# A four-layer block on one core: another order for the start-up work of the first two pairs

## The reference

```python
x = x + (x @ W0[expert[b]] + bias0[expert[b]])                         # 16 experts, one for a sample
x = x + (x @ W1.T + ((x @ A[ad[b]].T) @ B[ad[b]].T) * s[ad[b]])        # low-rank adapters, rank 16, 8 of them
x = x + attention(x)      # Wq, Wk, Wv, RMS norm, rotation by position, paged keys and values, window 256, Wo
x = x + (W3[subject[b]].T @ x + bias3[b])                              # mixes the 64 tokens of a sample
```

## Time and profile before

| | us |
|---|---|
| median of three runs | 952.81 |
| lowest and highest run | 951.57, 953.42 |
| span of the profiled execution (first to last instruction) | 948.6 |
| PE busy | 907.5 (96%) |
| DVE busy | 651.1 (69%) |
| POOL busy | 522.3 (55%) |
| ACT busy | 444.3 (47%) |

### The profile page before, as it was taken

How to read it: one execution, slowest core, us unless ns; L and a number is a source line. 1 busy time by engine, 2 the same in 40 slices (tenths; PEclk the granted TensorE clock), 3 DMA queues, 4 the chain that set the end, 5 groups by cost and what they waited for, 6 DMA issues and landing times.

```text
span 948.6 us, 23332 instructions
## 1 busy us (share of the span) xinstructions
PE 907.5 (96%) x6477; PEld 660.8 (70%) x6477; DVE 651.1 (69%) x1853; ACT 444.3 (47%) x1190; POOL 522.3 (55%) x502
## 2 busy tenths in 40 slices
PE   5789999999999999999997899999999999999997
PEld 3456666766666667666676777877777887787785
DVE  5345545667768774556754678777878877888875
ACT  2333333333333333333322566666666666666663
POOL 2136455464564657855556666566565665656530
PEclk9799999999999999999998799999999999999999
DMA  9978988778788787887844566666666676567741
GB/s 295 265 230 282 330 308 290 252 261 289 247 282 276 244 291 255 271 295 247 284 159 152 183 188 203 199 210 186 198 197 212 200 225 203 181 209 212 221 135 46
DMA packets 100413, 218.51 MB, mean 230 GB/s; under 512 B 30187, under 2 KB 36168, under 8 KB 92178
## 3 DMA queue, kind: packets, MB, share of 16 engines
q1 hardware_dynamic: 66290, 145.27, 47.0%
q0 software_dynamic: 25088, 57.74, 20.5%
q10 hardware_dynamic: 8992, 15.00, 4.9%
HBM read 210.39 MB, written 33.86 MB: 257 GB/s over the span
## 4 chain that ended last, share of the span: by engine, by line
PE 51%; POOL 18%; issue 15%; DMA 7%; SPq 4%; DVE 2%; ACT 1%; ACTq 1%; POOLq 0%; DVEq 0%
PE banks L823 9%; PE banks L775 9%; PE banks L811 7%; PE banks L798 6%; POOL rms L471 5%; DMA ring<-in_rope 5%; PE banks L752 4%; PE banks L859 3%; POOL ring L475 3%; POOL x_in L461 3%; PE banks L816 3%; POOL q_rot L480 2%; PE banks L753 1%; PE banks L791 1%; POOL ring L482 1%
## 5 line engine op out<-in xcount | busy, mean ns | idle before, releaser
L561 POOL DMA_INDIRECT ring<-new_rows,idx x128 | 129.4, 1011 | 82.5 <-PE banks L775 40.3
L471 POOL TENSOR_TENSOR rms<-ss,neg_half 128x12 f32<-128x12 f32 x31 | 70.8, 2284 | 185.4 <-DVE ss L1259 185.4
L992 ACT ACTIVATE big<-big,neg_max 128x320 f32<-128x320 f32 x256 | 141.4, 554 | 3.1 <-DVE neg_max L1317 2.7
L1317 DVE CUSTOM_DVE_ANT_0 big<-banks,mask 128x320 f32<-128x320 f32 x256 | 114.6, 486 | 27.4 <-PE banks L775 26.0
L602 PE MATMUL banks<-ring 128*64 128x512 f32 x512 | 117.8, 601 | 0.9 <-DMA ring<-in_w 0.9
L982 ACT ACTIVATE kt<-banks 128x384 f32<-128x384 f32 x128 | 61.8, 483 | 97.5 <-PE banks L753 97.5
L775 PE MATMUL banks<-kt,q_in 64*128 64x128 f32 (+2 forms) x768 | 88.6, 364 | 1.3 <-ACT kt L982 1.3
L550 POOL DMA_INDIRECT ring<-new_rows,idx x64 | 61.7, 965 | 47.0 <-PE banks L798 42.7
L1354 DVE TENSOR_SCALAR big<-big,recip 128x320 f32<-128x320 f32 x256 | 85.5, 396 | 2.3
L775 PEld LDWEIGHTS banks<-kt,q_in 64*128 64x128 f32 x768 | 74.4, 189 | 14.4 <-issue 8.4
L811 PEld LDWEIGHTS banks<-pt,ring 128*64 128x64 f32 x1024 | 55.4, 136 | 38.1 <-DVE pt L1299 25.4
(11 more groups left out here) (177 smaller groups left out, 1989.0 us busy)
## 6 DMA issues: line engine op xcount, KB each, us to landing
ring<-in_w SPq DMA_DIRECT2D x62, 1024.0 KB, 7.5
ring<-in_xt SPq DMA_DIRECT2D x32, 256.0 KB, 2.7
x_in<-in_x SPq DMA_DIRECT2D x32, 256.0 KB, 5.8
bias_in<-in_b SPq DMA_DIRECT2D x64, 128.0 KB, 6.4
x_dram<-x SPq DMA_DIRECT2D x32, 256.0 KB, 6.9
q_dram<-q_t ACTq DMA_DIRECT2D x32, 256.0 KB, 5.7
new_rows<-kv_out SPq DMA_DIRECT2D x32, 256.0 KB, 6.7
q_in<-q_dram SPq DMA_DIRECT2D x32, 256.0 KB, 2.7
```

The costliest lines, as they stand in the source:

```text
L471: nc.gpsimd.tensor_tensor(rms[:, s, :], ss[:, s, :], neg_half[:, :], ALU.pow).then_inc(rms_ready, 1)
L561: pool.indirect_dma_start(out=kv[:, s, c, :], out_offset=None, in_=new_rows, in_offset=bass.IndirectOffsetOnAxis(ap=idx[:, b, 1 + c:2 + c] ...
L992: nc.scalar.activation(prob[:, s % 2, PLACE[g] * NK:(PLACE[g] + 1) * NK], sm[:, s % 2, g, :], ACT.Exp, bias=neg_max[:, s % 2, g:g + 1], sc ...
L1317: V.tensor_tensor_reduce(sm[:, s % 2, g, :], ps_s[g], mask[:, s % 2, k0:k0 + NK], 1.0, 3.0e38, ALU.add, ALU.min, accum_out=neg_max[:, s % ...
```

## The change

Nothing is computed differently. What moves, engine by engine:

- ACT issues the B transfers of pair 0 at the very start, ahead of `w1_hi`; those of pair 1 go out at the end of step 0, behind `wqkv_hi` for the queries; the A copies of pair 1, `round_adapters(1)`, `wqkv_hi` for keys and values, and `take_adapters(2)` move from step 0 to step 1, behind `x2t_hi`.
- PE of pair 0 does the four high-by-high products of W1 first, then `adapt_down`, then waits for `w1_lo`, and waits for `x1t_lo` only ahead of the last four.
- DVE makes x2 of pair 0 without `split_adapters(1)` and `split_inputs(0)` ahead of it. These follow in step 1, behind `split_x2`: `split_inputs(0)`, `split_inputs(1)`, `split_adapters(1)`, and then the gains, which are no longer made at the start.

```diff
 PE   step 0
-                    if isinstance(k, int) and k < 2:
+                    if isinstance(k, int) and k == 1:
                         adapt_down(k, s)
...
-                        pe.wait_ge(w1_lo_ready, 1)
                     pe.wait_ge(x1hi_ready, k + 1)
-                    pe.wait_ge(x1lo_ready, k + 1)
+                    if not (isinstance(k, int) and k == 0):
+                        pe.wait_ge(x1lo_ready, k + 1)
                     for x_part, w_part in ((x1t_hi, w1_hi), (x1t_hi, w1_lo), (x1t_lo, w1_hi)):
+                        if isinstance(k, int) and k == 0 and w_part is w1_lo:
+                            adapt_down(k, s)
+                            pe.wait_ge(w1_lo_ready, 1)
+                        if isinstance(k, int) and k == 0 and x_part is x1t_lo:
+                            pe.wait_ge(x1lo_ready, 1)
 ACT  start
-            act.wait_ge(ld_w1, 16)
-            nc.scalar.activation(w1_hi[:, :, :], w1_stage, ACT.Copy).then_inc(w_hi_ready, 1)
...
             act.wait_ge(ld_ids, 16)
+            act.wait_ge(pb_set, 2)
+            take_adapters(0, 0, copy=False)
+            act.wait_ge(ld_w1, 16)
+            nc.scalar.activation(w1_hi[:, :, :], w1_stage, ACT.Copy).then_inc(w_hi_ready, 1)
             act.wait_ge(ld_small, 2 * 16)
-            act.wait_ge(pb_set, 2)
-            for k in range(2):
-                take_adapters(k, k, copy=False)
 ACT  steps 0 and 1
+                if isinstance(k, int) and k == 1:
+                    act.wait_ge(ld_wkv, 2 * 16)
+                    nc.scalar.activation(wqkv_hi[:, :, D:], wqkv_stage[:, :, D:], ACT.Copy).then_inc(w_hi_ready, 1)
+                    take_adapters(1, 1, load=False)
+                    round_adapters(1, 0, 1)
+                    take_adapters(2, 0)
...
-                    for n in range(2):
-                        take_adapters(n, n, load=False)
+                    take_adapters(0, 0, load=False)
...
-                if on(k, -1, NP):
+                if on(k, -1, NP) and not (isinstance(k, int) and k == 0):
                     round_adapters(k + 1, j + s, 1 - s)
...
-                if isinstance(k, int) and k == 0:
-                    act.wait_ge(ld_wkv, 2 * 16)
-                    nc.scalar.activation(wqkv_hi[:, :, D:], wqkv_stage[:, :, D:], ACT.Copy).then_inc(w_hi_ready, 1)
+                    take_adapters(1, 1, copy=False)
...
-                if on(k, -2, NP):
+                if on(k, -2, NP) and not (isinstance(k, int) and k == 0):
                     take_adapters(k + 2, s)
 DVE  start: the gains leave it
+            def make_gains():
+
+                link(V.tensor_scalar(gain_in[:, :, :], gain_in[:, :, :], 1.0, None, ALU.add))
...
 DVE  steps 0 and 1
                 if isinstance(k, int) and k == 1:
                     split_x2(k)
+                    split_inputs(0)
                     split_inputs(1)
+                    split_adapters(1, 1)
+                    make_gains()
...
-                if on(k, -1, NP):
+                if on(k, -1, NP) and not (isinstance(k, int) and k == 0):
                     split_adapters(k + 1, r)
-                if isinstance(k, int) and k == 0:
-                    split_inputs(0)
```

More of the change, by code:

```diff
@@ L1079, in _ @@
             link(V.tensor_scalar(beyond[:, :], odd[:, :], BIG, None, ALU.mult))
[L1080 to L1084, removed]
+            def make_gains():
+                link(V.tensor_scalar(gain_in[:, :, :], gain_in[:, :, :], 1.0, None, ALU.add))
+                for w, g in ((0, -1.0 / 16.0), (1, 1.0)):
+                    for f, half, sign in ((0, 0, 1.0), (1, 1, 1.0), (2, 1, -1.0), (3, 0, 1.0)):
+                        link(V.tensor_scalar(gains[:, w, f, :], gain_in[:, w, 32 * half:32 * half + 32], g * sign, None, ALU.mult))
+                V.tensor_copy(scol[:, 4:5], scol[:, 3:4]).then_inc(gains_ready, 1)
             def take_tables():
```

## The result

The changed kernel took 941.72 us (median of four runs, 940.94 to 944.5) beside 953.12 us of the kernel before: ratio 0.99, 95% interval 0.9882 to 0.9919. That is 11.4 us faster by the medians, and 9.5 (7.7 to 11.2) by the ratio. The forecast was 946.7, with 944.3 to 950.2 as its range: the sign was right, the gain nearly twice what was forecast, and outside the range. One profiled execution of the changed kernel took 942.46 us with a span of 940.7.

What follows compares the result with a forecast made beforehand. The prediction took PE's pace to bound both phases, so time gained at the start carries to the end. Pair 2's projections 6.9 us early, or 5.2 with half clock, middle 6.1: 952.8 - 6.1 = 946.7 us, range 944.3 to 950.2.

Steps and rivals of the forecast that it cites:

- step 5: Pair 1's experts wait for their second matrix, landing 14.1 us after issue; x1 at 41.3 against 48.88, 7.6 us left.
- step 3: x2 of pair 0 right behind h, at 25.3 (27.2 at half clock) against 34.93: 9.6 us (7.7) gained.
- Steps 6 and 7: Late gains put pair 0's tab at 38.1, load_in(2) 10.2 us later, pair 2's experts at 51.2; 5.0 us left.
- step 8: POOL's sum beside pair 2's experts; projections near 56.4 against 63.29, 6.9 us, or 5.2 with half clock; middle 6.1 taken.
- Step 1: Pair 0's B rows ahead of W1 make it land 0.6 us later; w1_hi runs from 17.7 to 19.6.
- Steps 2 and 3: Pair 0: h done at 24.6 (26.5 at half clock) against 28.91, then x2 at once, 25.3 (27.2).
- step 4: Pair 1's projections, bound by DVE's moved remainders, end at 34.2 (38 at half clock) against 44.5.
- the load of pair 2 isn't the limit: Rival: that load lands with PE or before, PE goes by x1 of pair 1; 944.3 to 945.2 us, chance 0.13.
- the clock takes more: Rival: two or three half-clock stretches at the start cost 1.7 us each; 948.8 to 949.8 us, chance 0.18.
- 4.2 us lie outside of it; I let them stand: Median 952.81 against profiled span 948.6 us; the difference was left and the gain subtracted from the median.
- slow load of pair 2: Rival: it lands in 14.1 us in place of 8.3; gain 1.1, 951.7 us; chance 0.14, including no effect.
- late B rows of pair 1: Rival: late landing holds gains, tab, load and pair 2's experts; with 18 us, 3.2 us slower, 956.0; chance 0.05.

Runs made afterwards that it cites:

- e7: Kernel before with only DVE's order changed: x2 of pair 0 made ahead of split_inputs(0) and split_adapters(1); 951.06 us, ratio 0.9985.
- e6: Kernel before with only the B transfers of both first pairs issued ahead of w1_hi; 945.22 us, ratio 0.9919.
- e3: Changed kernel with the gains made at the start again; 940.91 us, ratio 0.9869.
- e11: Changed kernel with B rows of both pairs and gains at the start, and POOL's sum of pair 2 ahead of the rotation; 938.79 us, ratio 0.985.
- e15: Changed kernel with the same three moves as e11, run again later; 938.63 us, ratio 0.9867.
- e9: Kernel before with dummy products keeping PE busy in its pauses of pair 0, to hold the clock up; 952.11 us, ratio 0.9987.
- e4: Changed kernel with pair 0's B transfers issued behind w1_hi, ACT's waits for ids and pb_set left ahead of it; 945.5 us, ratio 0.9916.
- e5: Changed kernel with pair 0's B transfers and ACT's waits for ids and pb_set behind w1_hi; 945.04 us, ratio 0.9929.
- e2: Changed kernel run again without any edit; 940.8 us, ratio 0.9882.
- e13: Changed kernel run again without any edit, later and beside e15; 943.28 us, ratio 0.9912.
- e1: Kernel before run again without any edit; 953.58 us, ratio 1.0011.

## Why the prediction was wrong in size and right in kind

**The step that failed is step 5, the wait for pair 1's second matrix.** It let only "7.6 us" of the start's gain pass, by landing that matrix 14.1 us behind its issue. It landed after 10.7 to 11.5 us, and x1 of pair 1 came 9.9 us earlier (48.9 in the mean of before's three profiles, 39.0 in changed's): nothing of the 9.6 us of step 3 was lost there. Steps 6 and 7 then sized the gains and the load too dear as well, and step 8, which missed a wait, gave back part of that by luck.

**Steps 1 to 3 held.** Step 1: `w1_hi` 17.38 us in the mean of before's three profiles, 18.14 in changed's, 0.8 later against 0.6 (0.6 too by the means of six above). Steps 2 and 3: x2 6.7 us behind `w1_hi` in every profile, against 6.9. But "here lies the gain of the start" names only half of it. Taking DVE's work away from x2 alone gave 1.0 us (e7), the B rows alone 6.8 (e6). The prediction read the chain of DVE and passed over the one of ACT, whose roundings of `wqkv` stood behind the wait for B rows.

**"So the moved remainders now bound the projections, and 9.6 is still there, within 1"** (step 4) held: the projections of pair 1 ended at 34.96 (36.67 less the wait of 1.71), 16.0 us behind `w1_hi`, against 16.5.

**Steps 5 to 7, too dear.** They put the experts of pair 2 at 51.2; in the mean of three profiles they began at 47.5. Four sizes, all above what was measured.
- "landed 14.1 us later": the second matrix of pair 1 took 11.5, 11.0 and 10.7 us from issue to landing, against 14.1, 13.8 and 14.4 in before. The text gave 34 as the other end, for want of `load_in(2)` beside it, and then used the row of the old queue. The landings were 36.2, 34.1 and 34.7, although the issue had moved too, to 24.7, 23.1 and 24.0 (5.8 us behind `w1_hi`, in before as in changed). But its reason is not the main one: with `load_in(2)` issued at 27.4 to 28.8 again the matrix took 11.9 us in e3, 11.4 in e6, 10.2 in e11 and 9.5 in e15. What goes with the long time is four B transfers issued behind `w1_hi`: 13.8 to 14.8 us in the five profiles that have it (before, e7, e9), 12.3 and 12.4 with only pair 0's there (e4, e5). e6 differs from before in these transfers alone. Why they cost so much is not shown.
- "10 instructions of 0.345 us": measured 2.1 us in all (0.22 + 1.70 and the copy of 0.15), not 3.4, and `tab` 0.72, not 1.14. The rows of before had been timed with POOL's sum beside the one and DVE's remainders beside the other.
- "landed 32.2": it was 32.5, but with a `w1_hi` 1.2 us later than assumed; counted from that, 13.6, 12.6 and 13.3 us in place of 14.5. The issues ran from 23.98 to 25.34, and the landing released ACT at 32.51, 7.2 us behind the last (6.2 and 6.9 in e2 and e13), so the row of 7.8 us was near. The prediction had set it against the Trainium skill's rule that a DMA engine takes turns between the rings (DMA: Bandwidth & Descriptors, section Queues, rings and completion order), by which the rows would land before DVE is free. Here they did, though not far ahead: DVE's remainders ended at 32.77, and it then waited 0.49 us for ACT's rounding (0.27 in e13, none in e2).
- "38.2 + 13.0": from the first issue of `load_in(2)` to the landing of its second matrix it took 12.5, 10.7 and 11.0 us. (The 48.9 beside it should be 48.7: from 48.88 to 56.24 is 7.4 us and not 7.6. Nothing hangs on it.)

From `w1_hi` to the projections of pair 2 the forecast came to 38.7, measured 37.3, 35.9 and 35.6.

**Step 8's "so it lies beside the experts now" was wrong.** POOL's sum ran at 52.94, when the experts were ending at 54.92, only because these were late and at half clock; in e2 and e3 x1 waited for the sum. From these experts to the projections the forecast had 5.2 us, and 6.6, 7.4 and 6.6 were measured. It made the load of pair 2 a near tie with the next limit, and so the rival "the load of pair 2 isn't the limit" could be true (e3) and still give nothing.

**"I take the middle, 6.1": 0.8 us.** In the changed kernel's first profile the half clock did come behind a wait, and cost 5.30 - 3.65 = 1.65 us of pair 2's experts; it was so in e13 too (5.35). In e2 they ran at full clock, and the first eight products of pair 2's projections took 3.24 us in place of 2.10. So the event was foretold, and its price on the experts right. But of the 1.65 only 0.7 us in the one and 0.1 in the other reached x1 of pair 2, as POOL's sum ended at 54.21 (experts at 54.92) and 52.44 (52.54) anyway. And before had such stretches as well (0.75 and 0.54 in the windows above), over all three profiles of each kernel the start differed by 9.8 us with the clock in it, and there was nothing to subtract. The rival "the clock takes more" failed with it.

**"4.2 us lie outside of it; I let them stand": 0.9 us, and the wrong way to read a profile.** The changed kernel's execution shows 1.8 us outside its span (942.46 - 940.7), and the others that gave both numbers 1.7 to 1.9. So the profiled execution of before had taken some 950.4, 2.4 less than its median (single executions of it ran from 948.9 to 958.5 in later sets), and part of that sits in the start: its projections of pair 2 came at 63.29, 0.9 earlier than the mean of three, 64.2. A gain reckoned from one execution that was early itself is that much too small.

The sum: forecast 6.1, plus 0.9 (before's early execution), plus 2.0 (54.4 in the mean, not 56.4: 3.7 by steps 5 to 7, less 1.7 by step 8), plus 0.8 (clock) is 9.8, which is the start's difference in the profiles. The three sets of runs gave 9.7 in the mean by the ratios and 10.6 by the medians; the 0.8 between is within the noise and isn't located. The stretch to the end varied between 883.4 and 887.4 in both kernels, and no experiment tells it from that spread.

**The other rivals.** The slow load of pair 2 (14.1 us) and the late B rows of pair 1 did not come: the former was 7.5 us from issue to landing against 8.3, and the B rows landed where the near row had them.

## What to carry to other kernels

Count each stage from the landing that starts it, over two or three profiled executions, before a gain of 1% is forecast: here the landing of W1 alone moved by 2 us, and a single execution stood 2.4 us from its median. A transfer, or an instruction, that was timed beside other traffic or a busy neighbour should be priced again for the neighbours it will have after the change. When a wait is removed and nothing moves, look for the next limit within a microsecond of it; three edits that each gave nothing measurable gave some 3.3 us together.

## What the runs showed of the hardware that was not expected

**DVE and POOL hold each other up.** The same eight products of the gains took 2.76 us when POOL's sum began 1.0 us into them (one of the eight took 1.24 us, the others 0.18), and 1.70 when it began behind them. Timeline of e1:

```profile
13.35 1.70 DVE L1083 TENSOR_SCALAR gains<-reals 128x32 f32<-128x32 f32 x8
...
15.38 1.26 POOL L461 TENSOR_TENSOR x_in<-x_in,bias_in 128x512 f32<-128x512 f32 x1 [6.97 <-DMA bias_in<-in_b]
...
38.65 2.28 DVE L1217 TENSOR_TENSOR wqkv_lo<-stage,wqkv_hi 128x2048 fp32r<-128x2048 f32 x1
39.08 2.99 POOL L461 TENSOR_TENSOR x_in<-x_in,bias_in 128x512 f32<-128x512 f32 x1 [11.63 <-DMA ring<-in_rope]
```

The other way round, POOL's sum took 1.26 us by itself and 2.99 beside DVE's remainder of 128x2048, whose own 2.28 was no longer than alone. Other executions gave 2.37 to 3.11 for that sum, and in all five it ended 1.1 to 1.2 us behind the end of DVE's instruction (42.07 and 40.93 here). In both cases the one that began later looks to have stood still until the other had ended, rather than both running slower. They were seen in the runs and not isolated by one of their own.

**The table load moves with the waits ahead of it.** In e4 three waits in a row stood ahead of the first activation, and its table load ran only when the last was over, at 19.26, so that `w1_hi` began 1.4 us behind the landing. In e5, with the wait for W1 alone ahead of it, the load ran at 1.63. Timeline of e4, then of e5:

```profile
19.26 1.28 ACT L901 ACT_TABLE_LOAD   x1 [19.12 <-DMA stage<-in_w]
20.55 1.91 ACT L901 ACTIVATE w_hi<-stage 128x2048 fp32r<-128x2048 f32 x1
```

```profile
1.63 1.28 ACT L899 ACT_TABLE_LOAD   x1 [1.50 <-PEq L1441]
...
19.27 1.91 ACT L899 ACTIVATE w_hi<-stage 128x2048 fp32r<-128x2048 f32 x1 [16.36 <-DMA stage<-in_w]
```

In the changed kernel, with two issues between the second and the third wait, it ran at 4.85. The times of e4 and e5 can't be told apart (0.9916 and 0.9929, intervals of some 0.2% either way), so what the late load costs isn't known.
